# Filler products in TensorE's waits, value copies and weights on SyncE's queue, and the shared expert's low parts on VectorE, in a two-layer kernel on one core

## The reference, cut to what matters

```python
q = rope(rms(x @ Wq.T)); k = rope(rms(x @ Wk.T)); v = x @ Wv.T
k_blocks = k_blocks.at[blk, :, off, :].set(k)      # new rows go into a paged cache
v_blocks = v_blocks.at[blk, :, off, :].set(v)
scores = einsum('bghtd,bgsd->bghts', qg, k_all) * SCALE
p = softmax(where(last 128 positions, scores, -inf))
x2 = einsum(p, v_all) @ Wo.T
logits = x2 @ Wr.T + bias ; the best 2 of 16 experts for each token
routed = sum over the 2 of w * (silu(x2 @ Wg[e]) * (x2 @ Wu[e])) @ Wd[e]
shared = silu(x2 @ sWg) * (x2 @ sWu) @ sWd
x = x + routed + shared
```

## Time and profile before

| | before |
|---|---|
| median of 3 runs | 584.53 us (583.47 to 586.75) |
| the profiled execution, its own time | 580.49 us |
| its span in the trace | 578.7 us |
| PE, DVE, ACT, POOL busy | 86%, 62%, 44%, 45% of the span |
| mean granted clock of TensorE | 0.931 |

### The profile page before, as it was taken

How to read it: one execution, slowest core, us unless ns; L and a number is a source line. 1 busy time by engine, 2 the same in 40 slices (tenths; PEclk the granted TensorE clock), 3 DMA queues, 4 the chain that set the end, 5 groups by cost and what they waited for, 6 DMA issues and landing times. The chain is left out here.

```text
span 578.7 us, 10881 instructions
## 1 busy us (share of the span) xinstructions
PE 495.7 (86%) x4207; PEld 375.7 (65%) x4207; DVE 359.3 (62%) x777; ACT 252.8 (44%) x548; POOL 261.9 (45%) x240
## 2 busy tenths in 40 slices
PE   2997799999998999998879899477999998199956
PEld 0686368886886788776644347356777775099846
DVE  2757478886686878845676555953466886334412
ACT  6287753343432444243872334363355544034420
POOL 5055435463443677775650000378572017445640
PEclk9799999999999999999999899756699999689987
DMA  5564681000000121230000009511000002498326
GB/s 172 185 253 171 263 242 42 1 1 1 0 1 1 37 71 57 68 102 16 2 3 1 1 1 353 192 40 26 14 26 5 3 1 82 158 332 257 112 71 195
DMA packets 24723, 51.53 MB, mean 89 GB/s; under 512 B 4264, under 2 KB 16705, under 8 KB 23520
## 3 DMA queue, kind: packets, MB, share of 16 engines
q1 hardware_dynamic: 18704, 40.62, 20.4%
q0 software_dynamic: 5968, 10.22, 5.9%
HBM read 43.99 MB, written 12.37 MB: 97 GB/s over the span
## 5 line engine op out<-in xcount | busy, mean ns | idle before, releaser
L753 PE MATMUL ps<-x_split,gate_up_split 128*128 128x512 f32 x384 | 96.3, 393 | 0.1
L753 PEld LDWEIGHTS ps<-x_split,gate_up_split 128*128 128x128 f32 x384 | 72.0, 188 | 17.1 <-issue 1.5
L2055 POOL DMA_INDIRECT wbig<-new_kv,prepi x40 | 42.4, 1059 | 79.8 <-DVE wmid L1443 68.7
L940 POOL TENSOR_TENSOR gate_up_split<-wbig,gate_up_split 128x768 fp32r<-128x768 f32 (+1 forms) x24 | 41.5, 1731 | 52.3 <-ACT gate_up_split L882 52.2
L864 DVE TENSOR_TENSOR hidden_split<-work,hidden_split 128x512 fp32r<-128x512 f32 x34 | 37.7, 1109 | 23.1 <-ACT hidden_split L929 23.1
L775 PE MATMUL ps<-hidden_split,down_split 128*128 128x512 f32 x160 | 42.5, 395 | 2.6 <-issue 1.4
L1995 POOL DMA_INDIRECT chosen<-work,wbig x31 | 30.5, 984 | 30.8 <-ACT work L1980 16.6
L929 ACT ACTIVATE hidden_split<-work 128x512 fp32r<-128x512 f32 x34 | 21.4, 630 | 50.6 <-DVE work L859 48.4
L946 POOL TENSOR_TENSOR down_split<-wbig,down_split 128x384 fp32r<-128x384 f32 (+1 forms) x24 | 29.1, 1213 | 25.9 <-ACT down_split L889 25.8
L2055 POOL DMA_INDIRECT wbig<-in_cache_dram,prepi x32 | 33.5, 1047 | 7.6 <-issue 6.9
L775 PEld LDWEIGHTS ps<-hidden_split,down_split 128*128 128x128 f32 x160 | 29.8, 188 | 10.7 <-issue 4.2
(11 more groups left out here) (337 smaller groups left out, 1180.1 us busy)
## 6 DMA issues: line engine op xcount, KB each, us to landing
work<-in_wE_dram SPq DMA_DIRECT2D x1, 5376.0 KB, 16.1
wbig<-in_wF_dram SPq DMA_DIRECT2D x3, 1664.0 KB, 7.0
sorted<-wmid SPq DMA_DIRECT2D x1, 3999.0 KB, 16.8
wbig<-in_wG_dram SPq DMA_DIRECT2D x1, 3072.0 KB, 10.3
wbig<-in_wE_dram SPq DMA_DIRECT2D x6, 384.0 KB
wbig<-chosen SPq DMA_DIRECT2D x8, 256.0 KB, 5.1
wbig<-sorted SPq DMA_DIRECT2D x1, 1935.0 KB, 12.8
wmid<-in_wE_dram SPq DMA_DIRECT2D x5, 384.0 KB
```

What stands on the lines that cost most here:

```text
L753: mm = nc.tensor.matmul(o, self.gus[:, w % 2, a, 2 * m + k, :], self.xs[:, b, k, n * HALF:(n + 1) * HALF], start=(k == 0 and a == b), stop ...
L940: nc.gpsimd.tensor_tensor(self.gus[:, k % 2, 1, 0:self.gu_chunks], self.gate_up[:, :, j * P:(j + 1) * P], self.gus[:, k % 2, 0, 0:self.gu_ ...
L2055: return nc.gpsimd.indirect_dma_start(dst, None, table, bass.IndirectOffsetOnAxis(ap=rows.bitcast(U32), axis=0), **({} if bound is None el ...
```

## The change

There are four parts.

1. `unread(n, bank)` issues n float32 products of the identity with `small[:, 0:512]`. Nobody reads them. It is called at eight places of TensorE's list: 2 products ahead of the fold transposes, 2 behind them, 9 between the two halves of query turns, 7 behind `keys(0)`, 2 behind `scores(1)`, 14 behind the shared expert, 7 behind a new wait for `sent`, and 15 between the last expert tile and the final sums; 58 in all.
2. `vlast` is cleared once by GpSimd. SP then copies each group's own 32-row pieces into its diagonal blocks (four transfers a group, 32 in all), and the expert weights are loaded behind them on SP's queue.
3. `keys(0)` no longer waits for `page_qm` and writes to banks 4 and 5; the wait moved into `scores(0)`. ScalarE keeps these keys after its query copies, as before.
4. The two low parts of the shared expert are computed by VectorE at the end of `route_vector`, ahead of its copies to `cT`.

```diff
+        KEY_BANK = lambda q4: (0, 1) if q4 else (4, 5)
+        def unread(n, bank):
+            for _ in range(n):
+                nc.tensor.matmul(ps[:, bank, :], ident, small[:, 0:512], start=True, stop=True)
...
+            pe.wait_ge(sem("page_v_raw"), 2)
+            unread(2, 3)
             pe.wait_ge(sem("page_raw"), 4)
...
             tr.then_inc(sem("fold_turned"), 1)
+            unread(2, 3)
             pe.wait_ge(sem("fold_kept"), 1)
...
-            pe.wait_ge(sem("page_qm"), 16)
-            pe.wait_ge(sem("page_table"), 10 + B // 4)
-            pe.wait_ge(sem("page_token"), 1)
+                if n == 0:
+                    unread(9, 3)
...
             def scores(b):
+                if b == 0:
+                    pe.wait_ge(sem("page_qm"), 16)
+                    pe.wait_ge(sem("page_table"), 10 + B // 4)
+                    pe.wait_ge(sem("page_token"), 1)
...
-                pe.wait_ge(sem("page_vlast"), q4 + 1)
+                pe.wait_ge(sem(f"page_vlast{q4 % 2}"), 16 * 4 * (q4 // 2 + 1))
...
             keys(0)
+            unread(7, 7)
             scores(0)
             for b in range(B + 2):
                 if b + 1 < B:
                     scores(b + 1)
+                if b == 0:
+                    unread(2, 7)
...
+            for k in moe.first_splits():
+                moe.lo_gate_up(dve, k, nc.vector)
+            moe.lo_down(dve, 0, nc.vector)
...
             pe.wait_ge(sem("ffn_h_ready"), moe.count("h_ready", 2))
+            unread(14, 5)
             pe.wait_ge(sem("ffn_out"), moe.count("out", 4))
             pe.wait_ge(sem("ld_wE_low"), 16)
+            pe.wait_ge(sem("sent"), 16 * 2 * NT)
+            unread(7, 5)
...
+            pe.wait_ge(sem("tile_h"), N_TILE)
+            unread(15, 0)
...
+            for q4 in range(B // 4):
+                sp.wait_ge(sem(f"overlay{q4 % 4}"), 16 * 5 * (q4 // 4 + 1))
+                if q4 == 0:
+                    sp.wait_ge(sem("page_token"), 2)
+                if q4 >= 2:
+                    sp.wait_ge(sem("page_pv"), q4 - 1)
+                for j in range(4):
+                    own = slice(32 * j, 32 * j + 32)
+                    sp.dma_start(vlast[own, q4 % 2, j, :], kv[own, B + q4, P:2 * P]).then_inc(sem(f"page_vlast{q4 % 2}"), 16)
+            by_expert = wE_d.rearrange("(e p) f -> p e f", p=P)
+            sp.dma_start(w_high, by_expert[:, LOW:NE + 1, :]).then_inc(sem("ld_wE"), 16)
+            sp.dma_start(w_low, by_expert[:, 0:LOW, :]).then_inc(sem("ld_wE_low"), 16)
...
+            pool.wait_ge(sem("page_ms"), 4)
+            nc.gpsimd.memset(vlast.rearrange("p r b f -> p (r b f)"), 0.0).then_inc(sem("page_token"), 1)
             pool.wait_ge(sem("page_new"), 32)
-            def last_values(q4):
...
-            moe.gpsimd(pool)
             experts_gpsimd(pool)
```

More of the change, by code:

```diff
@@ L935, in scalar, with lo_gate_up, lo_down @@
                         self.extra_scalar(act, i)
-            def lo_gate_up(self, pool, k):
+            def lo_gate_up(self, pool, k, engine=nc.gpsimd):
                 s, j = self.s, self.splits[k]
                 self.wait(pool, "gu_hi", k + 1)
-                nc.gpsimd.tensor_tensor(self.gus[:, k % 2, 1, 0:self.gu_chunks], self.gate_up[:, :, j * P:(j + 1) * P],
+                engine.tensor_tensor(self.gus[:, k % 2, 1, 0:self.gu_chunks], self.gate_up[:, :, j * P:(j + 1) * P],
                                         self.gus[:, k % 2, 0, 0:self.gu_chunks].bitcast(F32), ALU.subtract).then_inc(s("gu_lo"), 1)
-            def lo_down(self, pool, k):
+            def lo_down(self, pool, k, engine=nc.gpsimd):
                 s, j = self.s, self.splits[k]
                 self.wait(pool, "dn_hi", k + 1)
-                nc.gpsimd.tensor_tensor(self.dns[:, k % 2, 1, 0:self.dn_cols], self.down[:, j, :],
+                engine.tensor_tensor(self.dns[:, k % 2, 1, 0:self.dn_cols], self.down[:, j, :],
                                         self.dns[:, k % 2, 0, 0:self.dn_cols].bitcast(F32), ALU.subtract).then_inc(s("dn_lo"), 1)
@@ L1384, in program @@
         page_wo = cut(wpage, 1024, KC * (D + NE)).rearrange("p (c o) -> p c o", c=KC)
-        wo_turned = cut(wmid, 2048, 512).rearrange("p (c k) -> p c k", c=KC)
+        wo_turned = cut(wmid, 1280, 512).rearrange("p (c k) -> p c k", c=KC)
         LOGIT_BANK = 6
+        KEY_BANK = lambda q4: (0, 1) if q4 else (4, 5)
         gsc = small_buf(KC * PHD).rearrange("p (a f) -> p a f", a=2)
@@ L1483, in keys @@
                     pe.wait_ge(sem("page_kT"), 2 * q4)
+                main, last = KEY_BANK(q4)
                 for j in range(4):
-                    nc.tensor.transpose(ps[:, 0, j * P:(j + 1) * P], kv[:, 4 * q4 + j, 0:P], ident)
-                nc.tensor.transpose(ps[:, 1, 0:P], kv[:, B + q4, 0:P], ident).then_inc(sem("page_k"), 1)
+                    nc.tensor.transpose(ps[:, main, j * P:(j + 1) * P], kv[:, 4 * q4 + j, 0:P], ident)
+                nc.tensor.transpose(ps[:, last, 0:P], kv[:, B + q4, 0:P], ident).then_inc(sem("page_k"), 1)
             def scores(b):
+                if b == 0:
+                    pe.wait_ge(sem("page_qm"), 16)
+                    pe.wait_ge(sem("page_table"), 10 + B // 4)
+                    pe.wait_ge(sem("page_token"), 1)
                 pe.wait_ge(sem("page_kT"), 2 * (b // 4) + 2)
@@ L1667, in keep_keys @@
                     act.wait_ge(sem("page_scores"), 4 * q4 - 4)
-                nc.scalar.activation(kT[:, :, 0:P], ps[:, 0, :].rearrange("p (b j) -> p b j", b=4), ACT.Copy)\
+                main, last = KEY_BANK(q4)
+                nc.scalar.activation(kT[:, :, 0:P], ps[:, main, :].rearrange("p (b j) -> p b j", b=4), ACT.Copy)\
                     .then_inc(sem("page_kT"), 1)
-                nc.scalar.activation(kT[:, :, P:NKEY], ps[:, 1, 0:P].rearrange("p (b j) -> p b j", b=4), ACT.Copy)\
+                nc.scalar.activation(kT[:, :, P:NKEY], ps[:, last, 0:P].rearrange("p (b j) -> p b j", b=4), ACT.Copy)\
                     .then_inc(sem("page_kT"), 1)
@@ L2104, in _ @@
             sp.wait_ge(sem("lin_mem"), 4)
-            by_expert = wE_d.rearrange("(e p) f -> p e f", p=P)
-            sp.dma_start(w_high, by_expert[:, LOW:NE + 1, :]).then_inc(sem("ld_wE"), 16)
-            sp.dma_start(w_low, by_expert[:, 0:LOW, :]).then_inc(sem("ld_wE_low"), 16)
             for n in range(2):
```

8 lines of the change are left out of this document (removed).

## The result

The changed kernel took 606.71 us (median; 604.8 to 610.67), the kernel before beside it 584.66 us: a ratio of 1.0379, 95% interval 1.0334 to 1.0425. It is slower by 22 us. I had forecast 582.9 us with a range of 575 to 590, so both the value and the side were wrong. Ratios leave out the executions that the record calls slow (for the kernel before in experiment 8 one of 815.9 us at a mean granted clock of 0.56, beside a median of 567.24), and medians keep them, so a ratio can differ a little from the quotient of two medians.

What follows compares the result with a forecast made beforehand. TensorE was taken to bound the page loop, with low clock costing time there and behind idle spells. Terms -7.3 + 3.4 + 2.3 = -1.6 us took 580.49 to 578.9, by ratio 582.9 us; range 575 to 590.

Steps and rivals of the forecast that it cites:

- What one unread product costs: TensorE's filler products: two trace records each, 0.85 us at full clock and 1.71 us at half.
- The entry: Entry of the page loop: first scores +2.6 us, turn of group 1 +1.5 us (390.6 for 389.06).
- the earlier turn of keys: Entry of the page loop: `keys(0)` takes its 1.11 us and the wait ahead off the path, about 1.8 us.
- That is worth 0: none of the idle spells in the loop stands ahead of a turn of keys, so no gather was late: Page loop: GpSimd's first gather can start some 4 us earlier, which gains 0.
- The 32 small copies replace eight GpSimd operations off the path: 0: Page loop: copies for vlast cost 0, with a full round between a group's landing and its values.
- The loop, -8.8: Page loop, group 1 to 7: full clock, 7.8 us a round, 6.2 us of idle kept; 53.1 for 61.9 us.
- Rival 1: Page loop: the clock falls again once for 10 us, +3.4, 588.0 us; chance 0.23.
- Weights and low parts, 0: Loop's end and shared expert: weights land with six us of slack, low parts' VectorE cost is hidden; both 0.
- Ahead of the tiles, and of the sums: First tile's turn +5.0, clock saves 1.6, net +3.4; final sums start +5.1, save 2.8, net +2.3 us.
- Rival 5: The weights collide with the loop's end and the sends' start: +3, 587.5 us; chance 0.11.
- Rival 4: Unread products do not hold the clock, 1.71 us each: entry +18, tiles +20, sums +14, 637 us; chance 0.02.

Runs made afterwards that it cites:

- experiment 8: Set on a fourth chip, kernel before at 567.24 us; among others the changed kernel with only the unread products cut to the numbers of fit: 0.9878, and fit: 0.9948.
- old_values: The changed kernel with part 2 undone: GpSimd makes vlast by multiplications between gathers, weights loaded ahead of the new rows; 591.64 us, ratio 1.0144.
- no_copies: The changed kernel without the 32 transfers into vlast, SyncE's waits kept; 604.81 us, ratio 1.0395.
- after_again: The changed kernel itself, run again on a third chip where the kernel before took 568.42 us; 574.66 us, ratio 1.0113.
- before_again: The kernel before, unchanged, profiled once more on another chip; 567.13 us.
- fit: old_values with 27 unread products in place of 58; 562.65 us, ratio 0.988, in later sets 0.9897, 0.9948 and 0.9956.
- held: The changed kernel with GpSimd waiting, ahead of each five gathers from group 3 on, for scores of the group three before; 606.07 us, ratio 1.0419.

## Why the prediction was wrong

The span grew by 25.5 us: 2.6 of scatter ahead of the stage, 1.4 to the turn of group 1, 15.5 in the loop, 5.0 to the first tile, 3.6 to the sums, and -2.6 behind them.

- *What one unread product costs.* Right: 116 records, two to a product, and nine products take the 7.73 us from 372.71 to the next start at 380.44, 0.86 us each.
- *The entry.* Right: forecast +1.5 at the turn of group 1, measured +1.4 on either kind of chip. Without the unread products it is 36.4 for 38.4, so the earlier turn of keys wins about 2 us, where I had 1.8 (one profile each).
- *"That is worth 0: none of the idle spells in the loop stands ahead of a turn of keys, so no gather was late"*, and *"The 32 small copies replace eight GpSimd operations off the path: 0"*. **This is the step that failed.** No gather was late, but I had asked only whether the gathers' results come in time, and not what the gathers do to what runs beside them. Without the multiplications and their waits for the values GpSimd runs all 40 through; on a chip of this kind the others then stop for 4 to 12 us at a time. That term is 77.5 - 57.6 = 20 us of the loop and not 0 (the changed kernel against old_values; 18 us by no_copies, which shared its set, and 13 us in the whole time). The rows of before had the sign of it: every spell that I kept in the loop as given, 6.2 us, lies beside gathers, and behind the last gather, which ends at 436.1, only waits for VectorE or ScalarE are left, which after_again has too.
- *The loop, -8.8.* Wrong in size as well. With part 2 undone it won 61.9 - 57.6 = 4.3 us. All of the 8.8 was to come from the first two rounds, where the clock had been low: they fell from 28.3 to 22.6 us, 5.7. The other four went from 33.6 to 35.0, as rounds 2 to 5 now all took 9.1 to 9.2 us, where before two did: GpSimd and the values take turns there, and I had averaged those spells away into 7.8 us a round. Where there are no spells the loop went from 46.2 to 44.0.
- *Rival 1* had the right mechanism (the clock falls again beside group 0's values and the gathers), but one low stretch of 10 us for +3.4 where it was the stalls themselves, and half clock from 401 to 433. It was sized by the small spells of before, so no case of mine reached above 590 with a chance worth having.
- *Weights and low parts, 0.* Right. From the turn of group 7 to the start of the shared expert's last products it is 40.3 us in the traces of before and after, 43.2 and 43.3 in those of before_again and after_again. The two were not tried apart.
- *Ahead of the tiles, and of the sums.* Right: +5.0 was forecast for the first turn, measured +5.0 on either kind of chip in the one pair of profiles each; then +5.1 - 1.6 = +3.5 forecast to the sums, measured +3.6 and +3.3; then -2.8, measured -2.6 and -2.0. On the second kind these add up to 6.3 us, against 6.2 in the medians, and the entry and the loop nearly cancel (+1.4 and -2.1). `fit` shows the same from the other side: with fewer products it is 1.0% to 1.2% under the kernel before in two sets and 0.5% in a third, all on that kind, and within the scatter (0.9956, 0.9902 to 1.0009) on the first.
- *Rival 5* has a slip: its 587.5 adds the 3 us to the kernel before. Added to the forecast's -1.6 they give 585.9. Nothing hangs on it.
- *Rival 4* is out by the trace: TensorE did nothing but unread products from 372.71 to 380.6 and was granted 1.00 there, and again from 511.3 to 529.3 and from 580.63 to 593.5. In the trace of before the final sums, products with the identity too, had 0.52 from 565 to 571 and 1.00 from 571 to 575.4, as the prediction had worked out.

What stays open: why some sets show the spells (those of the first profiles and two more) and others do not (three). No chip served in two sets, so "kind of chip" is a name for what the kernel before shows in a set; it may be the chip or anything else that differs from one set to the next. Open too is by what the gathers stop the others: a late product, a late semaphore, or instructions that do not come (the rows say "remote" in `DVE L1592` and "issue" in `held`). Against the last of these speaks that the instruction queues of the trace of after move nothing between 372 and 432 us (the 1.67 MB moved there are all on the two data queues), while the stalls end at 400.75, 412.69 and 424.61. The size of a gather was not varied.

## What to carry to other kernels

Ask of a run of indirect transfers not only whether it is in time but what runs beside it. Here small idle spells that the profile could not explain, all beside the gathers, were their price (6.2 us in the loop), and they grew (to waits of 7.19, 10.79 and 10.32 us) when the change removed what broke the run up. Filler work in a wait must be counted by what the trace shows for one (two records here, 0.85 us), and fitted to the wait: where there were no stalls, about half the products gave 1.2% where all of them cost 1.1%. And measure on more than one chip before an idle spell is taken for a property of the kernel.

## What the runs showed of the hardware

- The same program ran its page loop in 44.0 us on one chip and 77.5 on another, 574.66 us against 606.71 in all. The kernel before has 46.2 and 61.9 us for it, 567.64 and 584.66 in all. In the changed kernel the loop's extra time lies beside its 40 gathers of 128 rows, 1.3 us apart on both; all other stages agree within 3 us.
- On the first kind TensorE, VectorE and ScalarE stood still together for 4 to 12 us at a time while GpSimd and its transfers went on with a DMA share of 0.10 to 0.12, and one clear of 0.2 us between each five gathers changed nothing (76.8 us for the loop against 77.5). Waits of GpSimd in the run, 0.95 to 8.87 us long, ended these stalls (`held`, no wait of TensorE in the loop over 2 us), but where its gathers then ran beside the 32 small products of `values`, those came in bits, with 9.9 us between them in all.
- A float32 product of 512 columns is two records, 0.85 us at full clock, and 7.9 us and 18.0 us of such products with the identity kept the granted clock at 1.00.
